# Expert loop of a mixture-of-experts stage: seven of 39 steps cut to 128 slots, slots given out by columns of 128, first bias loaded earlier

## The reference, cut to what matters

```python
gate_logits = x_flat @ gate_w.T
topk_vals, topk_idx = jax.lax.top_k(gate_logits, K)
topk_w = jax.nn.softmax(topk_vals, axis=-1)
comb = comb.at[jnp.arange(T)[:, None], topk_idx].add(topk_w)
for e in range(E):
    h = jax.nn.gelu(x_flat @ w1[e].T + b1[e], approximate=False)
    ...
```

## Time and profile before

| | us |
|---|---|
| median of three runs | 1466.11 |
| lowest, highest | 1464.83, 1468.82 |
| profiled execution, its own time | 1467.59 |
| its span, first to last instruction | 1465.5 |
| TensorE / VectorE / ScalarE / GpSimd busy | 1213.9 / 797.0 / 695.7 / 601.7 |

### The profile page before, as it was taken

How to read it: one execution, slowest core, us unless ns; L and a number is a source line. 1 busy time by engine, 2 the same in 40 slices (tenths; PEclk the granted TensorE clock), 3 DMA queues, 4 the chain that set the end, 5 groups by cost and what they waited for, 6 DMA issues and landing times. The chain is left out here.

```text
span 1465.5 us, 28035 instructions
## 1 busy us (share of the span) xinstructions
PE 1213.9 (83%) x9389; PEld 822.9 (56%) x9390; DVE 797.0 (54%) x1573; ACT 695.7 (47%) x1344; POOL 601.7 (41%) x490
## 2 busy tenths in 40 slices
PE   3979989834798799778987987842999999999993
PEld 1546657622234433443344334741888888888882
DVE  3865655444546574666567444771545454545451
ACT  3565444426667566756675664322333323232321
POOL 3977645210730083008000000102477777777761
PEclk7999999977899999989999999555999999999997
DMA  5755887941981298139604830795343444444437
GB/s 172 171 133 141 173 191 169 189 108 24 210 244 41 53 224 233 39 72 241 178 1 83 192 100 15 254 362 143 53 80 73 80 72 74 75 80 72 77 56 243
DMA packets 334344, 190.20 MB, mean 130 GB/s; under 512 B 277872, under 2 KB 314992, under 8 KB 332080
## 3 DMA queue, kind: packets, MB, share of 16 engines
q1 hardware_dynamic: 297040, 133.50, 38.1%
q0 software_dynamic: 24704, 54.34, 16.2%
q10 hardware_dynamic: 12512, 1.21, 0.8%
HBM read 64.85 MB, written 60.96 MB: 86 GB/s over the span
## 5 line engine op out<-in xcount | busy, mean ns | idle before, releaser
L2115 ACT ACTIVATE all_last_rows<-moe_hbank,moe_b1T 128x256 f32<-128x256 f32 x312 | 129.8, 472 | 268.1 <-PE moe_hbank L2026 259.7
L2026 PE MATMUL moe_hbank<-moe_rowT,l_w1T 128*128 128x256 f16 x1872 | 213.1, 275 | 11.2 <-DMA moe_rowT<-moe_ends 11.2
L2041 PE MATMUL moe_ybank<-l_w2T,moe_shared 128*128 x1872 | 210.6, 273 | 0.0
L2026 PEld LDWEIGHTS moe_hbank<-moe_rowT,l_w1T 128*128 x1872 | 184.3, 99 | 33.9 <-issue 11.5
L2041 PEld LDWEIGHTS moe_ybank<-l_w2T,moe_shared 128*128 128x128 f16 x1872 | 183.2, 98 | 21.2
L1175 ACT ACTIVATE block_probs<-block_bank 128x1024 f32<-128x1024 f32 (+1 forms) x192 | 144.5, 808 | 75.2 <-PE block_bank L937 62.6
L1955 POOL DMA_INDIRECT acc_scratch<-moe_ends,moe_whither x78 | 132.4, 1698 | 78.5 <-issue 49.3
L804 POOL COPY block_stack<-block_stack 128x512 f16<-128x512 f16 x16 | 10.6, 664 | 364.6 <-ACT block_stack L1159 364.6
L2291 DVE TENSOR_SCALAR moe_shared<-all_last_rows 128x2048 f16<-128x2048 f32 x39 | 48.1, 1234 | 172.3 <-ACT all_last_rows L2115 168.3
L1928 POOL DMA_INDIRECT moe_ends<-rows_scratch,moe_which x78 | 120.8, 1549 | 45.2 <-POOL moe_which L1924 31.7
L934 PE MATMUL block_bank<-block_qkT 128*128 128x512 f16 (+3 forms) x384 | 95.1, 335 | 46.2 <-issue 24.3
(11 more groups left out here) (365 smaller groups left out, 2539.5 us busy)
## 6 DMA issues: line engine op xcount, KB each, us to landing
front_raw<-in_L_ffn_w POOLq DMA_DIRECT2D x32, 512.0 KB, 5.0
w_turned<-block_qk SPq DMA_DIRECT2D x32, 512.0 KB, 3.7
w_parts<-front_raw_hi POOLq DMA_DIRECT2D x32, 256.0 KB, 5.1
w_parts<-front_raw_lo POOLq DMA_DIRECT2D x32, 256.0 KB, 5.8
l_w1T<-w_turned SPq DMA_DIRECT2D x8, 1024.0 KB, 11.2
l_w2T<-w_turned SPq DMA_DIRECT2D x8, 1024.0 KB, 12.7
front_shared<-in_x SPq DMA_DIRECT2D x8, 512.0 KB, 7.0
x_scratch<-conv_mixed SPq DMA_DIRECT2D x8, 512.0 KB, 3.9
```

The lines of the kernel that those rows point to most:

```text
L2026: last = pe.matmul(hbank[:, c, :], w1T[:, e, wp, k, c * P:(c + 1) * P], rowT[q][:, xp * CC + k, :], start=n == 0, stop=n == 5)
L2041: last = pe.matmul(ybank[q][:, t, :], (hid_hi, hid_lo)[hp][q][:, c, t * P:(t + 1) * P], w2T[:, e, wp, c, :], start=n == 0, stop=n == 3 * H ...
L2115: act.activation(hid[:, c, :], hbank[:, c, :], ACT.Gelu, bias=b1T[:, e, c:c + 1], scale=1.0 / (GAIN * GAIN)).then_inc(S["gelu_done"], 1)
```

## The change

The loop has 32 paired steps as before and then seven single steps of one column, 71 columns in place of 78. An expert's slots are given out as pairs of columns; a rest of at most 128 is one odd column. The odd columns take the single steps, and halves of unused pairs where single steps don't suffice or the other way round. This needs two running sums, more arithmetic in `keys` and in `group_experts`. The waits count columns. `all_tiles` lays out three steps, loops over six times four, and lays out the last 12. The first bias is loaded by SyncE in the token block, behind the gate weights. In the router ScalarE rounds the rows in halves and one turn ahead (`x_high`), stores a turn's weights at the end of the next turn's copies, and the last turn's before the one-hots; VectorE computes that turn's weights before `group_bases`. The slots for gathers beyond the last step are gone.

```diff
-GROUPS = TILES * TOPK // GT + E_N - 1
+PAIRED = TILES * TOPK // GT
+SINGLE = E_N - 1
+GROUPS = PAIRED + SINGLE
...
-    COLS = GROUPS * GT
+    COLS = PAIRED * GT + SINGLE
...
+        LOOPS = (PAIRED - 2 * AHEAD) // 4
...
+            for j in range(AHEAD):
                 step(j, j)
+            with eng.Fori(0, LOOPS) as i:
                 for r in range(4):
+                    step(i * 4 + (AHEAD + r), (AHEAD + r) % 4)
+            for j in range(AHEAD + 4 * LOOPS, GROUPS):
                 step(j, j % 4)
...
+        def columns(j):
+            return GT if paired(j) else 1
...
-                    for t in range(GT):
+                    for t in range(columns(j)):
                         sp.dma_start_transpose(rowT[q][:, :, t * P:(t + 1) * P], got[r][:, t, 0:2 * D]).then_inc(S[f"xT{q}"], 16)
...
-                all_tiles(pool, step, 1)
+                all_tiles(pool, step)
...
-                                last = pe.matmul(hbank[:, c, :], w1T[:, e, wp, k, c * P:(c + 1) * P], rowT[q][:, xp * CC + k, :],
+                                last = pe.matmul(hbank[:, c, own], w1T[:, e, wp, k, c * P:(c + 1) * P], rowT[q][:, xp * CC + k, own],
...
-                    for t in range(GT):
+                    for t in range(columns(j)):
                         n = 0
                         for c in range(HC):
...
-                        if a and i == 6:
-                            store_extra(a - 1)
...
-                        if i == 1:
-                            act.wait_ge(S["x_done"], (a + 1) * PER)
...
+                        if a == 0 and i in (1, 3):
+                            x_high(0, i // 2)
+                        if a + 1 < TURNS and i in (5, 7):
+                            x_high(a + 1, i // 2 - 2)
+                    if a:
+                        store_extra(a - 1)
                 exps(TURNS - 1)
-                act.dma_start(b1T[:, :, :], b1.rearrange("e (c p) -> p e c", p=P), allow_slow_non_contiguous=True).then_inc(S["bias_loaded"], 16)
+                store_extra(TURNS - 1)
...
-                    if a == 0:
-                        store_extra(TURNS - 1)
...
+                    dve.tensor_tensor(fits, prefix, each(least_e), ALU.is_ge).then_inc(plan, 1)
+                    dve.scalar_tensor_tensor(place, each(base_e), float(GS), prefix, ALU.mult, ALU.add).then_inc(plan, 1)
+                    dve.wait_ge(plan, n + 2)
+                    dve.tensor_tensor(fits, fits, each(odd_e), ALU.mult).then_inc(plan, 1)
+                    dve.wait_ge(plan, n + 3)
+                    dve.tensor_tensor(place, place, fits, ALU.add).then_inc(plan, 1)
...
+                token_weights(TURNS - 1)
                 done, upto = group_bases()
...
+        gate_loads.append((b1T[:, :, :], p["L1_ffn_b1"].rearrange("e (c p) -> p e c", p=P), b1_loaded))
```

More of the change, by code:

```diff
@@ L1818, in route_and_experts, with all_tiles, paired, first_column @@
         batch = (B - 1, *range(B - 1))
-        CONSTS, NARROWED = 12 + TURNS, 3
+        CONSTS, NARROWED = 15 + TURNS, 3
         KEYED, WHOLE = 4, 1.5 * 2.0 ** 23
-        def all_tiles(eng, step, apart=0):
-            for j in range(3):
+        LOOPS = (PAIRED - 2 * AHEAD) // 4
+        def all_tiles(eng, step):
+            for j in range(AHEAD):
                 step(j, j)
-            with eng.Fori(0, (GROUPS - 3) // 4 - apart) as i:
+            with eng.Fori(0, LOOPS) as i:
                 for r in range(4):
-                    step(i * 4 + (3 + r), (3 + r) % 4)
-            for j in range(GROUPS - 4 * apart, GROUPS):
+                    step(i * 4 + (AHEAD + r), (AHEAD + r) % 4)
+            for j in range(AHEAD + 4 * LOOPS, GROUPS):
                 step(j, j % 4)
+        def paired(j):
+            return not isinstance(j, int) or j < PAIRED
+        def columns(j):
+            return GT if paired(j) else 1
+        def first_column(j):
+            return j * GT if paired(j) else PAIRED * GT + (j - PAIRED)
+        def arrived(j, r, every):
+            if paired(j):
+                return (j - r) * (16 * GT // every) + 16 * GT
+            return 16 * GT * (PAIRED // every) + 16 * ((j - PAIRED) // every + 1)
         def image_copies(eng, copy, sem, parity):
@@ L2018, in up @@
                     q, e = r % 2, expert(j)
-                    pe.wait_ge(S[f"xT{q}"], (j - q) * 16 + 32)
+                    pe.wait_ge(S[f"xT{q}"], arrived(j, q, 2))
+                    own = slice(0, columns(j) * P)
                     for c in range(HC):
@@ L2071, in store_extra, with x_high @@
                                   extra[:, a * PER:(a + 1) * PER, :].bitcast(U32), allow_slow_non_contiguous=True).then_inc(S["extra_stored"], 16)
+                def x_high(a, half):
+                    ts = slice(half * PER // 2, (half + 1) * PER // 2)
+                    act.wait_ge(S["x_done"], a * PER + ts.stop)
+                    if a >= 2 and half == 0:
+                        act.wait_ge(S[f"x_stored{a % 2}"], 16)
+                    act.activation(xrow[a % 2][:, ts, 0:D], tok[a][:, ts, :], ACT.Copy, scale=GAIN).then_inc(S["x_hi"], 1)
                 def exps(a):
@@ L2114, in step @@
                         act.wait_ge(S["h_full"], j * (HC // 2) + (c // 2 + 1))
-                        act.activation(hid[:, c, :], hbank[:, c, :], ACT.Gelu, bias=b1T[:, e, c:c + 1],
+                        own = slice(0, columns(j) * P)
+                        act.activation(hid[:, c, own], hbank[:, c, own], ACT.Gelu, bias=b1T[:, e, c:c + 1],
                                        scale=1.0 / (GAIN * GAIN)).then_inc(S["gelu_done"], 1)
@@ L2207, in keys, with each @@
+                    dve.wait_ge(plan, n + 7)
+                    dve.scalar_tensor_tensor(odd_e[:, :], above_e[:, :], float(PAIRED * GT + ODD // P), odd_e[:, :], ALU.add, ALU.add).then_inc(plan, 1)
+                    dve.wait_ge(plan, n + 8)
+                    dve.tensor_scalar(odd_e[:, :], odd_e[:, :], float(P), odds_all[:, 0:1], ALU.mult, ALU.subtract).then_inc(plan, 1)
+                    dve.wait_ge(plan, n + 9)
+                    return n + 9, (pairs, odds)
                 def keys(n):
+                    def each(v):
+                        return v[:, :].rearrange("p (a e) -> p a e", a=1).to_broadcast((P, TILES, E_N))
```

169 lines of the change are left out of this document (104 added, 65 removed).

## The result

Before: 1467.46 us (1464.83 to 1470.73, four runs). After: 1431.49 us (1429.81 to 1436.5, four runs). The ratio is 0.9758, 95% interval 0.9731 to 0.9785: 36 us faster. The forecast was 48.6 us faster, 1417.5 with a range up to 1429: direction right, result 14 us above the forecast and 2.5 outside the range.

The account below looks back on a forecast made before the run. TensorE was taken to bound the expert loop, after a late start behind the router. The terms -13.9 - 35.8 + 2.9 - 1.8 = -48.6 us took 1466.11 to 1417.5 us; range from 1412 less 3 up to 1429.

Parts of the forecast that it names:

- First bias, turns, plan (-13.9): Ahead of the expert loop: moved bias -13.35, router turns -3.4, row weights -0.4, plan arithmetic +3.2; slots known 13.9 us earlier.
- Single steps (-35.8): End of the expert loop: seven steps of 128 slots take 5.36 us each in place of 10.48, saving 35.8 us.
- Rival A: Single up products paced by the weight load: 1424 us if half hides (chance 0.15), 1432 if none does (0.04).
- Waits for rows (+2.9): Last single steps: TensorE waits 2.9 us for gathered rows before up(35); bounds 0 and +9.
- Rival B: Single steps bounded by GpSimd's queue of scatters, 6.4 us a step: 7 us lost, 1424 us; chance 0.15.
- Rival C: Before the loop: late row-weight stores or a held store issue delay gathers to 1000-1005, 4 to 9 us lost; chance 0.12.
- Rival D: Expert loop: TensorE's clock stays at 1.2 GHz, each paired step costs 10.48 us more; with eight, 1501 us; chance 0.03.
- Rival E: End of the loop: no wait for rows and a tail at its bound of -4 give 1412 us; chance 0.11.
- Tail (-1.8): After TensorE's last matmul: one-column scatters end after 7.5 us against 9.3, saving 1.8 us; bounds 0 and -4.
- Bias on SyncE's queue at no cost: Token block: the bias's 8192 small packets behind the gate weights cost nothing; without cover some 5 us.

Follow-up runs that it names:

- e8: Changed kernel with expert 0's weights at constant addresses in the seven single steps and the gather of step j+4 ahead of the scatter of step j: 1418.83 us.
- e1: Changed kernel with expert 0's weights at constant addresses in up and down products of the seven single steps: 1422.96 us.
- e5: Kernel before the change with only the first bias moved to the token block: 1452.54 us.
- e4: Kernel before the change with all 39 up products 128 columns wide instead of 256, down products whole: 1444.73 us.
- e6: Changed kernel with five loop passes instead of six, then unrolled single and paired steps in turn: 1435.31 us.
- e12: Changed kernel with expert 0 at constant addresses in the single steps' down products only, and the gather of step j+4 ahead of scatter j: 1417.34 us.
- e7: Changed kernel with unrolled single and paired steps in turn and the expert's number loaded once per unrolled step: 1429.45 us, ratio to before 0.9717.
- e2: Changed kernel with expert 0's weights at constant addresses in the up products of the seven single steps only: 1430.20 us.

## Why the prediction was right or wrong

- **First bias, turns, plan (-13.9): right.** 13.9 and 14.6 us by the two traces of the changed kernel, from the router's first transposes (71.3 to 72.3 us in all eleven kernels with this front). Bias alone 12.4 against 13.35, the rest 1.5 to 2.2 against 0.6: two errors of 1 us that cancel. Logit copies stand 10.21, 11.23 and 10.21 us apart; the second took longer, since ScalarE's rounding waited 1.19 us for the store of rows.
- **Single steps (-35.8): wrong, and this is the miss.** The step that failed is "48 x 0.057 = 2.74. A step is 5.36 in place of 10.48". The rate itself was right: 56 ns, 2.68 us, and e8 gives 5.30 us a step. But the matmuls of the earlier trace rows have no register operation in front: their addresses are constant. The loop's addresses come from a register, and their price had no row of its own because 10.48 us of matmuls covered it. The forecast took a stretch of 48 matmuls from the code and priced matmuls only, where TensorE also issues 48 address operations and two loads of the expert a step. Measured: 4.3 + 0.7 + 2.8 = 7.9 us at the pace of the last steps, 15.4 us in the seven. Cutting a step's work to half left its queue work whole.
- **Rival A: near in size by chance, wrong in mechanism.** It had 1424 to 1432 at 0.19, and 1431.5 came. But only 8.8 us of the loss lies in the ups, the half price of A; it had nothing for the 5.2 in front of the products. And the weight load adds nothing at 128 columns: 48 fresh ones ran at 56 ns in e1 and e8. The Trainium skill (TensorE: Matmul & The Clock Gate, Back-to-back issue gap) has about 81 ns for such pairs. The changed kernel's mean of 83 ns looks like it, and isn't it: it is a mean of 56 and 124, and goes to 56 when the addresses are constant. Here the measurement decides.
- **Waits for rows (+2.9): hidden by the miss.** None came, as the slow steps covered the chain. With steps at 5.3 us (e1) there were 4.5 us, the first and largest in front of up(34), not up(35): the forecast had worked out step 35 and passed over step 34, whose gather also stands behind a paired scatter.
- **Rival B (GpSimd's queue): off in the changed kernel, there once the rest is gone.** In e8 the scatters are 4.5 to 5.0 us apart, as the forecast's 4.55, and cost 2.4 us at the end.
- **Rival C (stores): off, and e5 shows it was near:** without the reorder the last store held up the gather by 1 us.
- **Rival D (clock): off.** TensorE's granted clock was again 0.50 from 926 to 1006, the 1.2 GHz level, with the engine busy 44.1 of 80 us, and the pieces behind the first 13.33 us of the loop are 5.24 us, as in the earlier trace rows. The window of the last steps shows the full level with TensorE at work for 52.7 of 58 us:

```profile
1339.00:1397.00 58.00, 52.72 (x551) 43.46 (x549) 23.79 (x53) 17.53 (x56) 22.64 (x27) 1.00 0.30 48
```

- **Rival E (less lost): half there.** No wait for rows came, but the tail gave no more than was forecast.
- **Tail (-1.8): right.** 1397.37 to 1404.89 is 7.5 us. **Bias on SyncE's queue at no cost: right** as far as shown. SyncE's next DMA issues at 359.92, where it was 360.67 before. The router's first transposes start between 921.1 and 931.5 in the twelve kernels with it, at 924.27 and 925.51 without (before, e4), so a cost of a microsecond or two would not show there.

## What to carry to other kernels

When a change halves the work of a step, list all that the step's engine issues, not only its arithmetic: register loads, address operations for operands that a register picks, waits. What costs nothing under a long step is the bound of a short one, and the profile of the long step shows it only as instructions, not as time. Where short steps can't shed it, put them between long ones, whose cover the queue can use as a lead, load what can be kept only once (without that, e6 gained nothing), and then turn at once to the next chain (here the gather behind the scatter), or the gain will be a new wait.

## What the runs showed of the hardware that was not expected

- On TensorE a weight load behind an address operation follows the last such one after 0.124 us; with constant addresses weight loads and matmuls of 128 columns follow each other after 0.056 us (granted clock 1.00). From the start of a register load of the expert to the next weight load it takes 0.85 us.
- TensorE's queue gets ahead of its matmuls by a bounded amount. When a single up started right behind matmuls that had covered the queue, 7 to 10 of its 32 address operations were done (10 to 15 of its 48 matmuls), in e12 too, where the queue had time for more. That lead lasted for 24 to 37 matmuls at 56 ns. So the cost of register work depends on what runs before it: the same single up product took 3.2 (e12), 3.4 (e7) or 4.3 us (the changed kernel), by the work around it alone.
- Speeding up the queue work of one product sped up the other one (e2, e12).
